# A one-core decoder layer: cross attention fed by fewer, larger transfers, and its value products moved two steps behind the scores

## The reference, cut to what matters

```python
x = x + attn(layernorm(x))            # linear attention: no softmax
x = x + xattn(ctx, ctx, layernorm(x)) # what the change touches
x = x + ffn(layernorm(x))             # 16 routed experts and a shared one

def _feature_map(x, fm_w, fm_b):      # 8 features of a head become 16
    z = jnp.einsum('nshd,ed->nshe', x, fm_w) + fm_b
    return jnp.concatenate([jnp.exp(z), jnp.exp(-z)], axis=-1)
v, k, q = (_feature_map(x, fm_w, fm_b) for x in (v, k, q))   # 16 heads
scores = jnp.einsum('nqhd,nkhd->nhqk', q, k) / jnp.sqrt(128)
attn = jax.nn.softmax(scores, axis=-1)
out = jnp.einsum('nhql,nlhd->nqhd', attn, v)
return out.reshape(N, S, 256) @ fc_w.T + fc_b
```

## Time and profile before

| | |
|---|---|
| median of 3 runs | 672.51 us (663.89, 672.51, 672.90) |
| the profiled execution | 663.64 us, its span 661.8 us |
| PE busy | 474.3 us, 72% |
| DVE, ACT, POOL busy | 341.8, 253.9, 190.8 us |
| mean granted TensorE clock | 0.863 of full speed |
| moved by DMA | 61.94 MB in 101485 packets |

### The profile page before, as it was taken

How to read it: one execution, slowest core, us unless ns; L and a number is a source line. 1 busy time by engine, 2 the same in 40 slices (tenths; PEclk the granted TensorE clock), 3 DMA queues, 4 the chain that set the end, 5 groups by cost and what they waited for, 6 DMA issues and landing times.

```text
span 661.8 us, 11782 instructions
## 1 busy us (share of the span) xinstructions
PE 474.3 (72%) x3778; PEld 317.1 (48%) x3778; DVE 341.8 (52%) x969; ACT 253.9 (38%) x578; POOL 190.8 (29%) x223
## 2 busy tenths in 40 slices
PE   0588888777771259998888888859894188988860
PEld 0255555544441136665655656534562055766650
DVE  4567755616759325555675676464830032334343
ACT  0445545358780024333443444536630022323220
POOL 3132222357787000000000000011047600455560
PEclk9999999988885557677987899969897689899895
DMA  5820000003669998989898994000031101556639
GB/s 96 295 76 1 0 0 1 0 11 115 200 190 161 178 122 92 97 90 104 92 119 87 104 113 44 2 1 1 0 125 53 49 0 33 150 178 203 203 102 254
DMA packets 101485, 61.94 MB, mean 94 GB/s; under 512 B 33832, under 2 KB 99656, under 8 KB 101320
## 3 DMA queue, kind: packets, MB, share of 16 engines
q1 hardware_dynamic: 91976, 52.92, 45.9%
q0 software_dynamic: 2560, 5.31, 2.3%
q10 hardware_dynamic: 6912, 3.25, 2.1%
HBM read 40.34 MB, written 20.73 MB: 92 GB/s over the span
## 4 chain that ended last, share of the span: by engine, by line
PE 42%; DVE 15%; SPq 12%; ACT 8%; issue 8%; another core or an unknown queue 6%; DMA 6%; POOL 1%; ACTq 1%; DVEq 0%; POOLq 0%
SPq L473 5%; PE bank L711 4%; PE bank L696 4%; PE bank L1204 3%; PE bank L1214 3%; ACT prob L853 3%; PE bank L1215 2%; PE bank L1263 2%; PE bank L734 2%; DMA qst<-mT 2%; PE bank L740 2%; PE bank L666 2%; PE bank L728 2%; SPq L629 2%
## 5 line engine op out<-in xcount | busy, mean ns | idle before, releaser
L853 ACT ACTIVATE prob<-bank 77x512 f32<-77x512 f32 x128 | 73.5, 591 | 111.6 <-PE bank L696 111.1
L870 POOL COPY vcur<-vals 77x272 f32 (+1 forms) x32 | 13.2, 416 | 192.6 <-PE bank L711 192.6
L711 PE MATMUL bank<-prob,vcur 77*17 77x128 f32 x1024 | 58.6, 305 | 12.5 <-ACT prob L853 12.1
L1178 POOL DMA_INDIRECT routed<-t_y,t_no x48 | 45.9, 956 | 71.6 <-DVE t_y L1047 59.9
L778 DVE TENSOR_REDUCE mx<-bank 128x5 f32<-128x385 f32 (+1 forms) x96 | 53.6, 579 | 24.3 <-PE bank L666 22.4
L666 PE MATMUL bank<-kst,qst 96*128 96x77 bf16 x512 | 40.9, 225 | 32.8 <-DMA kst<-kparts 27.6
L696 PE MATMUL bank<-qst,kst 99*77 99x128 bf16 x512 | 57.9, 244 | 7.8 <-DMA qst<-mT 6.6
L696 PEld LDWEIGHTS bank<-qst,kst 99*77 99x77 bf16 x512 | 44.2, 132 | 18.3 <-issue 9.9
L825 DVE COPY avs_s<-bank 128x512 f32<-128x512 f32 x32 | 22.1, 692 | 59.2 <-PE bank L711 59.2
L941 DVE TENSOR_TENSOR act<-bank,s_g 128x512 f32<-128x512 f32 x24 | 16.5, 688 | 62.9 <-ACT s_g L1115 59.6
L666 PEld LDWEIGHTS bank<-kst,qst 96*128 96x128 bf16 x512 | 31.9, 115 | 35.6 <-DMA kst<-kparts 14.6
(11 more groups left out here) (178 smaller groups left out, 1066.6 us busy)
## 6 DMA issues: line engine op xcount, KB each, us to landing
qst<-qparts SPq DMA_DIRECT2D x96, 128.0 KB, 5.3
t_w<-in_expert_w SPq DMA_DIRECT2D x48, 192.0 KB
qparts<-qpart SPq DMA_DIRECT2D x16, 384.0 KB, 3.4
kparts<-kpart SPq DMA_DIRECT2D x48, 77.0 KB
kst<-kparts SPq DMA_DIRECT2D x16, 231.0 KB, 7.8
sorted_in<-fill SPq DMA_DIRECT2D x1, 3168.0 KB, 10.4
t_row<-sorted_in ACTq DMA_DIRECT2D x48, 66.0 KB
kst<-kparts SPq DMA_DIRECT2D x16, 154.0 KB, 8.1
```

Of the source, the lines that this page charges most:

```text
L711: i = pe.matmul(bank[4][32 * c:32 * c + EX + 1, (u - 1) * P:u * P], av_lhs(g, r, j, 4 * (u - 1) + c), prob[(u - 1) % 2][:, c], start=True, ...
L853: a.activation(prob[u % 2][:].rearrange("p c t -> p (c t)"), bank[2 + u % 2][0:KEYS], ACT.Exp, scale=SCORE_SCALE).then_inc(s["expd"], 1)
L1178: p.indirect_dma_start(out=routed, out_offset=bass.IndirectOffsetOnAxis(ap=t_no[r][:].bitcast(U32), axis=0), in_=t_y[r][:], in_offset=None ...
```

## The change

Four things change.

1. **The layout of the features.** A tile's 128 partitions are now 8 features of all 16 heads (`hf` 0 holds exp(z), 1 holds exp(-z)). `qparts` and `kparts` are stored by group of four sequences, with a part's (feature, head, token) contiguous. A feature's row in a group is then one run of 16 x 512 bf16 values (16 KB; 9856 bytes for the keys).
2. **The transfers.** All three parts of a tile leave in one transfer. `qst` and `kst` hold a group of four sequences instead of a pair, in three buffers instead of four (the third lies where phase 2's tiles were), filled by three transfers each. A transfer of `qst` with n copies of a part reads its source n times, through a source pattern whose outermost dimension has n entries with stride 0 (n is 3, 2 and 1). The first two groups are loaded from within phase 2. The shift's transfers go to POOL's queue.
3. **The attention.** No loop is left: 128 steps (`STEPS`) of four heads. Value products stand two steps behind the shifted scores (`LAG = 2`) and run on across the border of sequences, into bank 4 or 5 in turn, with three `prob` buffers; they read `vals` itself, so POOL's copies go. ACT instead of DVE copies the bank to `avs`. The scores run four sequences ahead. Bank 7 now takes the transposed shift, the transposes back and the final product.
4. **The bias.** POOL adds `fcb` to `xs` one sequence at a time instead of in one instruction, DVE writes the negated maximum directly, and a wait by a small copy per sequence goes.

The diff, cut to its core:

```diff
--- before.py
+++ after.py
-    NBUF = 4
+    NBUF = 3
...
-        qparts = nc.dram_tensor("qparts", (HEADS, EX, PARTS, TOK), BF16).ap()
-        kparts = nc.dram_tensor("kparts", (PARTS, EX, HEADS, B * KEYS), BF16).ap()
+        qparts = nc.dram_tensor("qparts", (NG, PARTS, EX, HEADS, GT), BF16).ap()
+        kparts = nc.dram_tensor("kparts", (NG, PARTS, EX, HEADS, JK), BF16).ap()
...
+            def sent(par, n):
+
                 for hf in range(2):
-                    heads = slice(hf * HALF, (hf + 1) * HALF)
+                    sp.wait_ge(q_sent[par][hf], n * 16)
+                    sp.wait_ge(k_sent[par][hf], n * 16)
+
+            def body(g):
+                par = g % 2
+                for hf in range(2):
                     sp.wait_ge(s["klo"], g * 2 + (hf + 1))
-                    for a in range(PARTS):
-                        sp.dma_start(kparts[a, :, heads, bass.ds(g * JK, JK)].rearrange("e h t -> h e t"),
-                                     kpart[par][hf][:, a]).then_inc(k_sent[par][hf], 16)
+                    sp.dma_start(kparts[g, :, hf * HD:(hf + 1) * HD].rearrange("a e h t -> (e h) a t"),
+                                 kpart[par][hf][:]).then_inc(k_sent[par][hf], 16)
                 for hf in range(2):
-                    heads = slice(hf * HALF, (hf + 1) * HALF)
                     sp.wait_ge(s["qlo"], g * 2 + (hf + 1))
-                    sp.dma_start(qparts[heads, :, :, bass.ds(g * GT, GT)].rearrange("h e a t -> (h e) a t"),
+                    sp.dma_start(qparts[g, :, hf * HD:(hf + 1) * HD].rearrange("a e h t -> (e h) a t"),
                                  qpart[par][hf][:]).then_inc(q_sent[par][hf], 16)
...
+
+            for g in range(NG):
+                if g < NG - 2:
+                    sp.wait_ge(s["ctxTp"], g + 1)
+                    ctx_load(g + 2, g % 2)
+                if g == 2:
+                    sent(0, 1)
+                    load_q(sp, 0)
+                if g == 3:
+                    load_k(sp, 0)
+                if g == 5:
+                    sent(1, 2)
+                    load_q(sp, 1)
+                if g == 6:
+                    load_k(sp, 1)
+                body(g)
...
+        stage = [sb3, sb3, early()]
+        qst = [place(f"qst{i}", [SHIFT_ROWS, HEADS, GT], BF16) for i, place in enumerate(stage)]
+        kst = [place(f"kst{i}", [SHIFT_ROWS, HEADS, JK], BF16) for i, place in enumerate(stage)]
...
-                for i in range(n):
-                    sp.dma_start(qst[r][(at + i) * EX:(at + i + 1) * EX],
-                                 qparts[:, :, part, bass.ds(g * JA * S, JA * S)].rearrange("h e t -> e h t")).then_inc(parts_in[r], 16)
+                same = qparts[group, part].rearrange("(o e) h t -> o e h t", o=1).broadcast_to([n, EX, HEADS, GT])
+                sp.dma_start(qst[r][at * EX:(at + n) * EX], same).then_inc(parts_in[r], 16)
+
+        def load_k(sp, group):
+
+            r = group % NBUF
             for at, part, n in K_RUNS:
                 sp.dma_start(kst[r][at * EX:(at + n) * EX],
-                             kparts[part:part + n, :, :, bass.ds(g * JA * KEYS, JA * KEYS)].rearrange("a e h t -> (a e) h t")).then_inc(parts_in[r], 16)
+                             kparts[group, part:part + n].rearrange("a e h t -> (a e) h t")).then_inc(parts_in[r], 16)
 
         def sp_phase3(sp):
-            def shift(g, r):
-                sp.wait_ge(s["mT"], g + 1)
-                for j in range(JA):
-                    at = j * (PARTS + 1) * HEADS
-                    sp.dma_start(qst[r][ROWS:SHIFT_ROWS, :, j * S:(j + 1) * S], mT[r % 2][at:at + PARTS * HEADS]).then_inc(m_in[r], 16)
-
-            def step_a(g, r, gb):
-                if g == 0:
-                    shift(g, r)
-                    load_parts(sp, 2, 2)
-                    all_sent(sp, NG // 2)
-
-            def body(g, r, gb):
-                if not is_last(g, 3):
-                    if not (is_first(g)):
-                        sp.wait_ge(s["bp"], g * (4 * JA))
-                    load_parts(sp, g + 3, (r + 3) % NBUF)
-                if not is_last(g, 1):
-                    shift(g + 1, (r + 1) % NBUF)
-            loop3(sp, body, step_a)
+            all_sent(sp, NG // 2)
+            sp.wait_ge(s["vp"], NG)
+            load_q(sp, 2)
+            load_k(sp, 2)
+            for group in range(3, NG):
+                sp.wait_ge(s["bp"], (group - 2) * (2 * 4 * JA))
+                load_q(sp, group)
+                load_k(sp, group)
...
+                if u == 0 and b % JP == 0:
+                    pe.wait_ge(parts_in[r], loads(b // JA))
+                if n >= 2:
...
+            def shifted(n):
+                b, u = n // 4, n % 4
+                g = b // JA
+                r, t = home(g, b % JA)
+                if u == 0 and b % JA == 0:
+                    if g == 2 * (NBUF - 1):
+                        pe.wait_ge(s["ones_rows"], 1 + NBUF)
+                    pe.wait_ge(m_in[r], shifts(g))
+                if n >= 2:
+                    pe.wait_ge(s["expd"], n - 1)
+                for c in range(4):
+                    h = 4 * u + c
+                    i = pe.matmul(bank[2 + n % 2][0:KEYS, c * S:(c + 1) * S],
+                                  kst[r][0:SHIFT_ROWS, h, t * KEYS:(t + 1) * KEYS],
+                                  qst[r][0:SHIFT_ROWS, h, t * S:(t + 1) * S], start=True, stop=True)
+                i.then_inc(s["bp"], 1)
+
+            def attend(n):
+                b, u = n // 4, n % 4
+                pe.wait_ge(s["expd"], n + 1)
+                if u == 0 and b >= 2:
+                    pe.wait_ge(s["avs"], b - 1)
+                for c in range(4):
+                    i = pe.matmul(bank[AV_BANK[b % 2]][32 * c:32 * c + EX + 1, u * P:(u + 1) * P],
+                                  vals[:, b, 4 * u + c], prob[n % 3][:, c], start=True, stop=True)
+                i.then_inc(s["avp"], 1)
...
+            def turn_back(b):
+                pe.wait_ge(s["avn"], b + 1)
+                if b > 0:
+                    pe.wait_ge(s["x2"], b)
+                pe.wait_ge(s["mT"], min((b + 2) // JA + 2, NA))
...
+            for n in range(STEPS):
+                b, u = n // 4, n % 4
+                shifted(n)
+                if n >= LAG:
+                    attend(n - LAG)
+                if u < len(UNITS) and b + JP < B:
+                    scores(b + JP, u)
+                if u == 0 and b % JA == 0 and b // JA + 1 < NA:
+                    turn_shift(b // JA + 1)
+                if u == 1 and b >= 2:
+                    turn_back(b - 2)
+                if u == 2 and b >= 2:
+                    project(b - 2)
+                if u == 3 and b >= 1:
+                    turn_values(b - 1)
...
+            for b in range(B):
+                for u in range(len(UNITS)):
+                    if b + JP < B:
+                        maxima(b + JP, u)
+                if b >= 2:
+                    add_attention(b - 2)
+                if b >= 1:
+                    divide(b - 1)
+                if b >= 2:
+                    statistics(b - 2)
+                if b % JA == JA - 1 and b + JP < B:
+                    parts((b + JP) // JA)
...
+            def copy_values(b):
+                a.wait_ge(s["avp"], 4 * b + 4)
+                if b > 0:
+                    a.wait_ge(s["tavp"], b)
+                a.copy(avs[:], bank[AV_BANK[b % 2]][:]).then_inc(s["avs"], 1)
...
+            for n in range(STEPS):
+                b, u = n // 4, n % 4
+                exponentials(n)
+                if u == 0 and b % JA == 0 and b // JA + 1 < NA:
+                    copy_shift(b // JA + 1)
+                if u == 1 and b >= 1:
+                    copy_values(b - 1)
+                if u == 1 and b >= 2:
+                    copy_back(b - 2)
...
+            def add_bias(b):
+                p.tensor_tensor(xs[:, b], xs[:, b], fcb[:], ALU.add).then_inc(s["xb2"], 1)
...
+            def shift(g):
+                p.wait_ge(s["mT"], g + 1)
...
+                    p.dma_start(qst[r][ROWS:SHIFT_ROWS, :, c * S:(c + 1) * S], mT[g % 2][at:at + PARTS * HEADS]).then_inc(m_in[r], 16)
+
+            p.wait_ge(s["xn2"], NG)
+            for b in range(JA):
+                add_bias(b)
+            shift(0)
+            all_sent(p, NG // 2)
+            p.wait_ge(s["vp"], NG)
+            p.wait_ge(s["xb2"], JA)
+            p.memset(kst[NBUF - 1][ROWS:SHIFT_ROWS], 1.0).then_inc(s["ones_rows"], 1)
+            p.wait_ge(s["ones_rows"], 1 + NBUF)
+            for g in range(1, NA):
+                shift(g)
                 for j in range(JA):
...
-
-            p.wait_ge(s["v_ready"], 2 * NG)
-
-            def copy_values(b, k):
-                p.tensor_copy(vcur[k][:], vals[:, bass.ds(b, 1)].rearrange("p o h e -> p (o h) e")).then_inc(s["v_cur"], 1)
-            for b in range(2 * JA):
-                copy_values(b, b)
-            p.wait_ge(s["xn2"], NG)
```

(12 more changed lines are left out.)

338 lines of the change are left out of this document (131 added, 207 removed).

## The result

The changed kernel is slower: 737.0 us in the median of four runs (727.47 to 754.03), against 669.6 for the kernel before; the ratio is 1.091 with a 95% interval from 1.075 to 1.108. Some executions of one kernel take a few per cent longer at a lower granted clock, and the ratios that have an interval leave these out, which is why 1.091 stands here and not the 1.101 of the medians. The forecast was 669, its range 638 to 712. The profiled execution took 741.3 us, its span is 739.5.

What follows compares the result with a forecast made beforehand. The bound was PE, its clock and the gap ahead of it. First exponential at 244, one group to 269, five load-paced periods to 398.5, then 423.5 and 441 against 436: +5 on 663.64 gives 669 us, range 638 to 712.

Steps and rivals of the forecast that it cites:

- The few engines: New `qst` loads: three- and two-fold repeated sources lie on 3 and 2 engines, the third and those of `kst` on 16.
- The rate of an engine: Group loads: 24.5 GB/s per engine taken between 26.2 and 23.3, lower end 19.5; 599,808 B last 24.5 us.
- L: A group's load from permission to landing: 26.8 us, with ends of 25.2 and 33.1 us.
- C: PE's time for a group in phase 3: 25 us with one 12 us low-clock stretch, 20 at full clock.
- the start: First exponential, the start of phase 3: near 244 us, bounds 241 and 255.
- Phase 2's stalls: Phase 2: ACT waits behind sends held by loads, 12.6 us at the fifth group and 14 at the eighth.
- The first shift's issue and landing (3 us): Between the features' end and the first exponential: the first shift adds 3 us.
- rival three: Phase 3: shifts wait behind large rows on three engines, 46 us over 14 pairs; 715 us, chance 0.11.
- The clock: Phase 3: one stretch of 12 us at 1.2 GHz in each group, behind a stall at its start.
- Rival two: Phase 3: the clock never recovers, all eight groups take 33.2 us; +74, 737 us, chance 0.11.
- The wait at the shift's transpose: Phase 3: PE's transpose of the shift right behind the pair adds some 1.25 us of wait per pair.
- Rival one: Loads spread over 16 engines at 419 GB/s, 4 us each, phase 2 runs free; 625 us, chance 0.10.

Runs made afterwards that it cites:

- e1: The changed kernel with each repeated-source load of `qst` split into n transfers of 16 rows, on sixteen engines; ratio to the kernel before 1.072, 718.75 us.
- e13: The changed kernel with the copies reordered in the stack, so a load's few engines write partitions that don't share a way; ratio to the kernel before 1.055.
- e14: e5 with the second group's load behind all sends, plus PE waiting at each group's second step for 14 POOL fills; ratio to the kernel before 1.090.
- e5: e1 with the rows of `qst` and `kst` reordered, so each transfer writes 16 partitions 6 apart; ratio to the kernel before 0.927.
- e12: e5 with LAG = 1, value products one step behind the shifted scores; ratio to the kernel before 0.941, four runs from 628 to 671 us.
- e4: The changed kernel with the shift's transfers on ACT's queue in place of POOL's; ratio to the kernel before 1.272.

## Why the prediction was wrong

**The few engines** were read rightly: e1 differs in that alone, and the first exponential came 24 us earlier.

**The rate of an engine is the step that failed.** The prediction took 24.5 GB/s "between 26.2 and 23.3" and 19.5 as the lower end, from transfers that write 128 partitions. A row alone did run at 26.5. But rows of two of the three engines share a way into SBUF (e13 undoes it), and those of `kst` share theirs among some four (an estimate from e1's 2.2 us in place of 0.61 for a row). From the permission (SP's issue at 291.30, 355.11 and 421.67 us) to the landing the load took 35.8, 39.5 and 35.6 us in place of 26.8, beyond even the bound of 33.1. The row that would have said so stood in the earlier trace rows: 0.81 of sixteen engines' time for 84 GB/s, which is 6.5 GB/s an engine, a quarter of the 26.2 of the earlier trace rows. I read it as demand that is met; it was a narrow way.

The form of the sum held. With 37 us for L, (C + L) / 2 gives 31.0 us for a group in place of 25.9, and the five that the loads were to pace took 32.3 each (first exponentials at 293.3 and 454.9 us). These five are 32 of the 43 us by which phase 3 exceeds the forecast's 197, and the start is 22 us late.

**Phase 2's stalls** were right in mechanism and too short: 21.35 and 20.80 us of ACT's idle time in place of 12.6 and 14. They hit the fifth and the eighth group, as forecast. The last copy of values begins at 240.3; the features were to end near 227.

**"The first shift's issue and landing (3 us)"** failed: 13.58 us, behind the third group's load, which SP issues at 250 us just ahead of it. This is rival three's mechanism; it was priced as a rival and left out of the sum. Within phase 3 of the change PE waits 12.4 us for shifts, in five waits and not in each of 14 pairs; in e1 it is the largest wait, 33.9 us.

**The clock.** One low stretch of 12 us per group was assumed; phase 3 ran at 0.63, about 178 of its 240 us at the low level, or 22 us per group. This isn't to be added to the loads' share: where PE waits for a load, a faster PE would wait longer. Rival two had all of it low, and its 737 us agree with the result by chance: there were full-clock stretches, and the first exponential came 22 us later than its start of 244. In e14 eight waits of 5.9 us in the mean were followed by 38 us more of PE's busy time, 4.8 us for each.

**C = 20 us at the full clock** was right (4 x 5.06). The comparison was not: I held 4.99 us against it as the old price, the shorter of the two sequences of a pair, where the pair's mean is 5.58. The wait at the shift's transpose is 0.88 us at the full clock (e5, PE's line 685 at 313.66 us); 1.25 was forecast.

**Rival one** gave 625 us for loads that spread over 16 engines, with 419 GB/s. Spread over the engines alone they gave 1.072. With the rows spread over SBUF too, the ratios of 0.927 to 0.960 make 621 to 643 us of the 669.6: its number was nearly right and its condition incomplete. That is partly luck, since such a load takes 14 us and not its 4.

## What to carry to other kernels

Ask of each transfer not only how many engines carry it but which partitions they write at the same moment. A high busy share of the engines at low GB/s was the sign of a narrow way here (0.82 at 86 GB/s, 0.35 at 88 once the rows were spread). Making transfers larger then lengthens the time for which everything queued behind them waits. A small transfer that a busy engine waits for belongs ahead of the large loads in their own queue, or the loads must be short. Add to the price of a stall of TensorE the low clock behind it (38 us for 49 us of idle time in e14), and don't count on the full clock where there is no stall (e12).

## What was not expected of the hardware

- The order of the rows, 16 partitions that lie 6 apart in place of adjacent ones, doubled a load's rate (126 to 254 GB/s).
- PE stayed at the low clock for 74 us in which it was busy for 72.65 (e12).
- A 12 KB transfer on ACT's queue waited 30 to 31 us for a load on SP's queue, in each of five groups of e4; the same on POOL's queue took 13.6 us at most. The Trainium skill, "DMA: Bandwidth & Descriptors", section "Queues, rings and completion order", has an engine go round its queues packet by packet; POOL's fits that better than ACT's does.
- Phase 4, which the change doesn't touch, took 191 to 195 us on one chip and 228 to 239 on the others.
